# Second attention: each head's operands stacked on 64 partitions, and transposes issued just ahead of the weighting

## What is computed

```
q = xn @ wq.T + bq;  k = xn @ wk.T + bk_;  v = xn @ wv.T + bv      # 8 x 512 x 256
scores = einsum('bhsd,bhtd->bhst', q, k) / sqrt(16)                # per batch and head 512 x 512
attn = softmax(scores, axis=-1)
out = einsum('bhst,bhtd->bhsd', attn, v)
return out @ wo.T + bo
```

## Time and profile before

| what | value |
| --- | --- |
| median of 3 runs | 2060.38 us (2059.51 to 2063.23) |
| profiled execution, its own time | 2060.63 us |
| its span in the trace | 2058.9 us |
| PE busy | 1896.0 us, 92% |
| DVE busy | 1444.2 us, 70% |
| ACT busy | 1283.8 us, 62% |
| POOL busy | 649.4 us, 32% |

### The profile page before, as it was taken

One profiled execution on the slowest core, in us unless ns is written; L12 is line 12 of the kernel. 1 busy time (PEld: TensorE's weight loads), 2 busy tenths in 40 slices (PEclk: granted clock), 3 DMA queues, 4 the chain that ended last, 5 costly groups with the idle time before them and its releaser, 6 DMA issues. The chain is left out here.

```text
span 2058.9 us, 33528 instructions
## 1 busy us (share of the span) xinstructions
PE 1896.0 (92%) x12080; PEld 1468.2 (71%) x12080; DVE 1444.2 (70%) x2916; ACT 1283.8 (62%) x3061; POOL 649.4 (32%) x1021
## 2 busy tenths in 40 slices
PE   1999999999999999999999699975999999999997
PEld 1888878778878788888888588863656655655653
DVE  5786885977858858868678554425777777777773
ACT  3665674665756746657567564532677777777784
POOL 0353453543534535535435232222001011111112
PEclk9999999999999999999999899996999999999999
DMA  6110211111112111111111474302001011011001
GB/s 226 42 42 22 52 42 32 42 32 44 40 32 50 43 33 42 32 42 42 28 35 42 132 273 151 113 26 93 21 1 52 1 52 52 1 52 52 1 32 42
DMA packets 75748, 112.34 MB, mean 55 GB/s; under 512 B 8256, under 2 KB 49600, under 8 KB 75072
## 3 DMA queue, kind: packets, MB, share of 16 engines
q1 hardware_dynamic: 75040, 109.14, 18.1%
q10 hardware_dynamic: 544, 1.05, 0.2%
HBM read 55.64 MB, written 20.97 MB: 37 GB/s over the span
## 5 line engine op out<-in xcount | busy, mean ns | idle before, releaser
L1519 DVE TENSOR_REDUCE nm<-ps 128x1 f32<-128x512 f32 x512 | 336.8, 687 | 117.4 <-PE ps L1382 112.7
L1626 ACT ACTIVATE pt<-pst 128x512 f32<-128x512 f32 x512 | 296.9, 602 | 143.2 <-PE pst L1390 141.7
L804 POOL TENSOR_SCALAR pr<-pr,rinv 128x128 f32<-128x128 f32 (+3 forms) x512 | 264.1, 537 | 374.3 <-DVE rinv L692 374.3
L572 ACT ACTIVATE pr<-sc,nmax 128x128 f32<-128x128 f32 (+3 forms) x512 | 268.5, 527 | 143.4 <-DVE nmax L681 141.9
L681 DVE TENSOR_REDUCE nmax<-sc 128x1 f32<-128x128 f32 (+3 forms) x512 | 222.9, 483 | 76.7 <-PE sc L408 76.7
L1382 PE MATMUL ps<-kb,qb 96*128 96x512 f32 x512 | 238.9, 468 | 13.5 <-DVE nm L1519 11.1
L810 POOL TENSOR_TENSOR qk<-ra,rb 128x256 f32<-128x256 f32 x256 | 183.5, 739 | 206.6 <-DVE rb L703 170.8
L1390 PE MATMUL pst<-qb,kb 128*128 128x512 f32 x512 | 208.1, 408 | 6.7 <-ACT pt L1626 3.6
L1382 PEld LDWEIGHTS ps<-kb,qb 96*128 96x128 f32 x512 | 97.9, 192 | 145.4 <-issue 83.8
L420 PE MATMUL w<-ident,pr 128*128 128x128 f32 x1280 | 171.3, 281 | 25.7 <-DVE rb L703 19.8
L382 PE MATMUL w<-wq_hi,xt_hi 128*128 128x384 f32 x512 | 183.0, 358 | 2.4 <-DVE xt_lo L675 1.5
(11 more groups left out here) (205 smaller groups left out, 4558.5 us busy)
## 6 DMA issues: line engine op xcount, KB each, us to landing
k<-k SPq DMA_DIRECT2D x256, 128.0 KB, 2.2
raw<-in_w SPq DMA_DIRECT2D x16, 640.0 KB, 5.7
raw<-in_w SPq DMA_DIRECT2D x8, 704.0 KB, 4.2
xa<-in_x SPq DMA_DIRECT2D x2, 2048.0 KB, 13.8
x<-in_x SPq DMA_DIRECT2D x8, 512.0 KB, 3.9
x_scratch<-x SPq DMA_DIRECT2D x8, 512.0 KB, 2.9
xt_hi_scratch<-xt_hi SPq DMA_DIRECT2D x1, 4096.0 KB, 14.0
xt_lo_scratch<-xt_lo SPq DMA_DIRECT2D x1, 4096.0 KB, 22.9
```

The source lines that it names most:

```text
L572: act.activation(pr[:, h, SOFF[i]:SOFF[i] + (i + 1) * P], sc[:, bank, at:at + (i + 1) * P], ACT.Exp, bias=nmax[:, h, i:i + 1], accum_out=r ...
L804: pool.tensor_scalar(p, p, rinv[:, h, i:i + 1], 1.0, ALU.mult, ALU.mult).then_inc(scaled, 1)
L1519: dve.tensor_reduce(nm[:, g % 2, i, h:h + 1], ps[:, i % 2, :], AXX, ALU.max, negate=True).then_inc(max_done, 1)
L1626: act.activation(pt[:, g % 2, h, i, :], pst[:, i % 2, :], ACT.Exp).then_inc(exp_done, 1)
```

## The change

- S4 = 64: a head's stack gets a fourth 16-row part, in front. In `zq` it is zero, in `zk` it holds ones in two columns (set once by POOL), which takes over the work of `sel`. So two heads fill 128 rows, and each head has a 64-row half of its own in `qb` and in `kb`. `own` and `sel` and their setup go.
- `score` and `score_t` contract over 64 rows, the half of their head: `slice(h % 2 * S4, h % 2 * S4 + S4)`. In a pair the two stand in opposite halves, since their heads are h + 1 and h.
- ACT copies four stacks per group instead of six. DVE's `take_n` adds the turned maxima to all 128 rows of `qb` instead of copying 32 rows.
- PE's transposes no longer stand between pairs, but behind pair (h,3), ahead of `weigh`: `turn_z` j = 2, 3 of group q + 2 at the end of step 0, `turn_o` at the end of step 1, `turn_z` j = 0, 1 of group q + 3 at the end of step 3. `turn_n` stays.
- DVE's `take_o` moves from after (1,3) to after (2,0).
- The projections stand after all four pairs of step 2 of g = 1. `turn_on` moves to the end of step 2 of g = 2, with ACT's copies at (3,0), (3,1) and `split_ot` at (3,2). `out_project`, `take_out` move to step 2 of g = 3. POOL's `finish` stands after the split of g = 3. `on` gets a second buffer.

```diff
-    S3 = 3 * D1
+    S4 = 4 * D1
...
-        TURNS = ((0, 0), (0, 1), (0, 3), (1, 1))
-        STACKS = ((0, 0), (0, 1), (0, 3), (1, 0), (1, 1), (1, 2))
-        PROJECTIONS = ((1, 3), (2, 0), (2, 2), (2, 3))
+        STACKS = ((0, 0), (0, 1), (1, 0), (1, 1))
+        PROJECTIONS = ((2, 0), (2, 1), (2, 2), (2, 3))
...
+                pool.memset(zq[:, :, :, 0, :].bitcast(F32), 0.0).then_inc(pads_set, 1)
+                pool.memset(zk[:, :, :, 0, :].bitcast(F32), 0.0).then_inc(pads_set, 1)
+                pool.wait_ge(pads_set, 2)
+                for a in range(2):
+                    pool.memset(zk[:, :, 2 * a:2 * a + 2, 0, 2 * a:2 * a + 2].bitcast(F32), 1.0).then_inc(pads_set, 1)
...
-                        if g == 2 and not first:
+                        if g == 3 and not first:
                             finish(b - 1)
...
                 def score(q, g, h, i):
-                    if h < 2 and i == 0:
-                        pe.wait_ge(stack_done, 6 * q + (3 if h == 0 else 6))
+                    if h % 2 == 0 and i == 0:
+                        pe.wait_ge(stack_done, 4 * q + 3 + h // 2)
                     n = 16 * q + 4 * h + i
+                    rows = slice(h % 2 * S4, h % 2 * S4 + S4)
                     pe.wait_ge(max_done, n)
-                    pe.matmul(ps[:, i % 2, :], qb[0:2 * S3, g, h // 2, i * P:(i + 1) * P], kb[0:2 * S3, g, h, :],
+                    pe.matmul(ps[:, i % 2, :], qb[rows, g, h // 2, i * P:(i + 1) * P], kb[rows, g, h // 2, :],
                               start=True, stop=True).then_inc(s_done, 1)
 
                 def score_t(q, g, h, i):
                     if h == 0 and i == 0:
                         pe.wait_ge(n_done, 2 * q + 2)
                     n = 16 * q + 4 * h + i
+                    rows = slice(h % 2 * S4, h % 2 * S4 + S4)
                     pe.wait_ge(exp_done, n)
-                    pe.matmul(pst[:, i % 2, :], kb[:, g, h, i * P:(i + 1) * P], qb[:, g, h // 2, :],
+                    pe.matmul(pst[:, i % 2, :], kb[rows, g, h // 2, i * P:(i + 1) * P], qb[rows, g, h // 2, :],
...
-                            if (h, i) in TURNS and more2:
-                                j = TURNS.index((h, i))
-                                if j < 2 and g == 2 and not first:
-                                    bank_read = (ot_lo_done, NC * b)
-                                elif j < 2 and g == 3 and not first:
-                                    bank_read = (so_done, NT * b)
-                                else:
-                                    bank_read = (stack_done, 6 * (q + 2) + (-2, 0, 1, 2)[j])
-                                turn_z(q + 2, j, bank_read)
                             if (h, i) in PROJECTIONS and projects:
                                 if (h, i) == PROJECTIONS[0]:
                                     pe.wait_ge(xs_in, 32 * b + 64)
                                     pe.wait_ge(z_lo_done, 2 * q + 6)
                                 project(b + 1, PROJECTIONS.index((h, i)))
-                            if h == 1 and i == 2 and back2:
-                                turn_o(q - 2, q + 1)
-                            if h == HG - 1:
-                                if i == 1 and more1:
-                                    turn_n(q + 1)
-                                if g == 1 and not first and i >= 2:
-                                    if last:
-                                        pe.wait_ge(stack_done, 6 * (q + 2) + 3 + i)
-                                    else:
-                                        pe.wait_ge(qn_done, 2 * NT * (b + 1) + 5 + i)
-                                    turn_on(b - 1, i - 2)
-                                if g == 2 and not first:
-                                    if i < 2 and not last:
-                                        pe.wait_ge(stack_done, 6 * (q + 2) + 5 + i)
-                                    out_project(b - 1, i)
+                            if h == HG - 1 and i == 1 and more1:
+                                turn_n(q + 1)
+                            if h == 2 and g == 3 and not first:
+                                if i < 2 and more2:
+                                    pe.wait_ge(stack_done, 4 * (q + 2) + 3 + i)
+                                out_project(b - 1, i)
+
+                        if h == 0 and more2:
+                            for j in (2, 3):
+                                turn_z(q + 2, j, (stack_done, 4 * (q + 2) + j - 1))
+                        if h == 1 and back2:
+                            turn_o(q - 2, q + 1)
+                        if h == 2 and g == 2 and not first:
+                            for k in range(NC):
+                                if more2:
+                                    pe.wait_ge(stack_done, 4 * (q + 2) + 3 + k)
+                                turn_on(b - 1, k)
+                        if h == HG - 1 and more3:
+                            for j in range(2):
+                                if projects:
+                                    bank_read = (qn_done, 2 * NT * (b + 2))
+                                elif g == 2 and not first:
+                                    bank_read = (ot_lo_done, NC * b)
+                                elif g == 3 and not first:
+                                    bank_read = (so_done, NT * b)
+                                else:
+                                    bank_read = (stack_done, 4 * (q + 2) + 3 + j)
+                                turn_z(q + 3, j, bank_read)
...
-                        dve.tensor_copy(qb[2 * S3:P, g, a, :], pn[2 * D1 * a:2 * D1 * (a + 1), :]).then_inc(n_done, 1)
+                        dve.tensor_tensor(qb[:, g, a, :], pn[:], qb[:, g, a, :].bitcast(F32), ALU.add).then_inc(n_done, 1)
...
-                            if h == 1 and i == 3 and back2:
+                            if h == 2 and i == 0 and back2:
                                 take_o(q - 2, (g + 2) % NG1)
+                            if h == 2 and g == 3 and not first:
+                                take_out(b - 1, i)
                             if h == HG - 1:
                                 if i == 1 and more1:
                                     take_n(q + 1, (g + 1) % NG1)
-                                if g == 1 and not first and i == 3:
+                                if g == 2 and not first and i == 2:
                                     split_ot(b - 1)
-                                if g == 2 and not first:
-                                    take_out(b - 1, i)
...
-                    rows = slice(0, 2 * S3)
-                    if j < 2:
-                        act.wait_ge(z_turned, 4 * q + j + 1)
-                        act.copy(qb[rows, g, j, :], w[rows, j, :]).then_inc(stack_done, 1)
-                    else:
-                        h = j - 2
-                        act.wait_ge(z_turned, 4 * q + 3 + h // 2)
-                        act.mul(kb[rows, g, h, :], w[rows, h // 2, :], own[rows, h % 2:h % 2 + 1]).then_inc(stack_done, 1)
+                    act.wait_ge(z_turned, 4 * q + j + 1)
+                    act.copy((qb, kb)[j // 2][:, g, j % 2, :], w[:, j % 2, :]).then_inc(stack_done, 1)
```

76 lines of the change are left out of this document (29 added, 47 removed).

## The result

The changed kernel takes **2206.9 us** (median of 4 runs, 2197.9 to 2212.7) against 2061.6 for the kernel before (4 runs, 2059.5 to 2063.2): ratio **1.070, 95% interval 1.066 to 1.074**. It is 7% slower. The prediction had the direction and most of the mechanisms; its time, 2122, and its range up to 2152 were too low. The profiled execution has a span of 2202.4 and a time of 2204.7.

The account below looks back on a forecast made before the run. Plain steps were taken as bound by a loop through DVE (or ACT) and PE. Per full batch 8.2 us, 10.2 with the clock, 61 over batches 1 to 6, total +62 on 2060.6: 2122 us, range 2098 to 2152.

Parts of the forecast that it names:

- the sum's 8.2: Added time per full batch without the clock: 0.5 + 0 + 1.5 + 6.2 us for g = 0 to 3.
- Pairs start together: `score` and `score_t` in opposite 64-row halves: starts 0.10 us apart, saving 0.24 once per step.
- Step 2 at 3.93: Plain step 2: 3.54 - 0.24, plus 0.63 for DVE's `take_o` between its first two maxima; +0.4 us.
- Step 3 of g = 3 and POOL: DVE's third `take_out` waits for POOL's `finish`, behind the split; steps 2 and 3 together +5.7 us.
- Step 3 of g = 2 and split_ot: PE's `turn_z` waits for `split_ot`, behind `take_n` and a maximum on DVE: 5.4 us instead of 2.4, +3.0.
- 2.6 + 0.3 + 0.4 + 0.53 + 1.00: Plain step 0, last `score_t` at 2.6, then two turns ahead of the weighting: 4.8 us, +0.1.
- +0.1, hidden by `take_n`: Plain step 3: two turns ahead of the weighting make 2.4 us where `take_n` and a maximum set 2.3.
- 4 x (2.03 + 0.34): Step 2 of g = 1: four projections with pairs, plus 0.25 + 1.0, giving 10.7 us; group change about 0.
- The switch of rows: Rival: array drains at switches around pairs, 16 us in all, 2138; chance 0.18 together with pairs not overlapping.
- The clock: Falls of the granted clock in g = 3 and often g = 2, 1.4 and 0.6 us, raising 8.2 to 10.2.
- the clock falls in plain groups too: Rival: a fall costing 1.4 us in every second group makes 22 us, 2144; chance 0.12.
- Start and end: Program start -1.5 us from fewer copies, batch 0 +1, batch 7 +2.

Follow-up runs that it names:

- e4: Changed kernel with the earlier kernel's order put back in every engine, keeping its stacks, copies and 64-row halves: 2053.5 us, ratio 0.9964 to the kernel before.
- e2: Changed kernel with DVE's `take_o` issued behind the fourth maximum of step 1 again: 2174.8 us, ratio 1.055 to the kernel before.
- e1: Changed kernel with POOL's `finish` ahead of the next group's low parts in g = 3: 2184.3 us, ratio 1.059 to the kernel before.
- e3: Changed kernel with `score` and `score_t` over all 128 rows, so no row halves (scores differ): 2158.0 us, ratio 1.047 to the kernel before.
- e6: Changed kernel with the first three `score_t` of each step 2 and step 3 issued twice: 2194.8 us, ratio 1.066 to the kernel before.

## Why the prediction was wrong in size

The direction was right, and so were the two waits in their place and cause. Three terms of the sum failed. The transposes behind the last pair and the pairs among full-row products are most of the 4.7 us a batch by which all but the clock came out above the sum's 8.2. The clock cost some 6.1 a batch where it had 2.0. The start, batch 0 and the end cost 27 where it had 1.5. Point by point, by its own steps:

- **Pairs start together.** Right, and more so: 0.00 apart, where I took 0.10. e4 shows the gain as worked out, 0.24 a plain step.
- **Step 2 at 3.93.** Right to 0.01, and its cause too: e2 takes `take_o` out and 0.62 goes.
- **Step 3 of g = 3 and POOL.** The mechanism was right. DVE waited 4.96 with POOL as releaser, and step 3 took 10.28 against my 8.6. From start to start, `turn_n` took 1.04 where it takes 0.68 at full clock, the last pair 0.56 (0.48), the two transposes 1.90 (1.02) and the weighting 1.28 (1.00). That is 1.6, and without it the step has 8.7. e1 confirms the wait: 4.5 less.
- **Step 3 of g = 2 and split_ot.** Right: from the end of the second maximum 6.5 instead of my 5.4, of which 0.85 + 0.47 are the lower clock.
- **The switch and the transposes: mis-sized.** This is the first step that failed. In "2.6 + 0.3 + 0.4 + 0.53 + 1.00" the last `score_t` came at 2.69, from it to the turn took 0.43, and two turns 1.02 instead of 0.93; in step 1 it was 2.19, 0.43 and 0.59 against 2.1, 0.3 and 0.53. Each of these steps came out 0.25 to 0.35 above my number, and the plain group at +1.3 instead of +0.5. Of step 3, "+0.1, hidden by `take_n`" had the wrong cover: it is 0.25 longer by `score`, 4.44 against 4.19 in the rows below, and e4 shows that without the two turns it is 1.02 shorter from weighting to weighting. The order costs 0.07 + 0.49 + 0.63 + 1.02 = 2.2 a plain group, in steps 0 to 3 (e4 to after).

  The first `score` of step 3 of g = 0 and that of the next step, in the kernel before:

```profile
1680.13 0.50 PE L1382 MATMUL ps<-kb,qb 96*128 96x512 f32 x1
...
1684.32 0.47 PE L1382 MATMUL ps<-kb,qb 96*128 96x512 f32 x1 [0.53 <-DVE nm L1519]
```

- **A lone pair: wrong.** "4 x (2.03 + 0.34)" has 2.37 for each cycle, and it took 2.70 to 2.72, since a pair among projections takes 0.62 to 0.64 (2.70 or 2.72 less the 2.08 of a projection) and not 0.34: step 2 of g = 1 took 11.8 and not 10.7, and the group is 1.6 longer and not 0. In step 2 of g = 3 it is the same: the last `score_t` came 4.0 after the first `score` and not 3.2, with cycles of 1.33 (pair to output projection 0.43, six products 0.90, where I had some 0.7), and the step took 6.3 and not 5.2. The two steps together are 2.2 a batch, some 13 in six.
- **The switch of rows,** which I priced at 16 in all as a rival's term, is behind both points: e3, without it, has each of these places shorter by 0.06 to 0.15. Pair to pair takes 0.33, pair to transpose or projection 0.42 to 0.43, and a transpose of four between pairs 0.59 where two in a row take 0.43 for the second: 0.1 on one side and 0.16 on the other. The Trainium skill, TensorEngine Tiling, Key Properties, says that a change of tiling mode drains the engine. The traces agree that such a change costs time; that it is a drain no run shows. The Trainium skill, TensorE: Matmul & The Clock Gate, Part 3, has products of different row groups starting about 4 ns apart. The traces agree: 0.00 to 0.01 us here. I had given the second only a place in the range and the first only a rival, where both hold at once.
- **The clock: wrong.** I took 2.0 a batch, in the shadow of two waits. In the batch shown the clock is at its lower level for 17.1 us: 6.8 in g = 2 and 10.2 in g = 3. The six batches have 0.91 over 575.93 us. A fall that meets eight transposes costs 0.9 by them alone (1.87 instead of 1.02), and falls hit steps 0 of g = 2 and g = 3 whose waits are no longer than those of g = 0 (0.55 and 0.3). That is the rival "the clock falls in plain groups too", given 0.12, in part: in plain steps of g = 2 and g = 3, while g = 0 and g = 1 of this batch have 1.00. e3 and e6, which give PE more work, have fewer falls. My argument against it was one window of the earlier trace rows with 0.82 busy at clock 1.00; g = 0 of the changed kernel has 14.81 of 17.69 busy, 0.84, and no fall either, so a busy share over a group did not tell where the clock falls. What does stays open.
- **Start and end: wrong.** I had -1.5 at the start, +1 for batch 0 and +2 for batch 7. The first weighting comes 4.6 later, the rest of batch 0 takes 7.3 more, batch 7 up to its last weighting 12.3 more and what follows 2.9 more. The clock is 0.50 from 1420 to 1460 and from 2160 to 2180 (before, 0.50 to 1.00 in the former). e3, with clock 0.66 to 1.00 there, has its first weighting 4.1 earlier than the kernel before. That the clock is all of it is argued, not shown.

The sum a batch: step 0 of g = 2 and of g = 3 took 1.6 more than the 5.14 of g = 0, and the two steps 3 had 1.3 and 1.6 of lower clock, 6.1 in all, where I had 2.0. What is left, 95.6 - 6.1 - 76.6 = 12.9, stands against my 8.2: +0.8 in g = 0, +1.6 in g = 1, +0.6 in g = 2, +1.7 in g = 3. These 8.8 us in six batches are 53 of the 81 us missed (143.5 more in span, where I had 62). Start, batch 0 and batch 7 make 26 more, and the first of the six batches was 2.6 longer than the one shown.

## What to carry to other kernels

Where a step is a loop through two engines, ask of each moved instruction on which side of the last product it lands: behind the last pair `turn_o` cost a step 0.17 or 0.49 more than between the pairs, and step 3 paid 1.02 for two transposes, while in a step without slack between the pairs moving them there gave nothing. In this kernel, sharing the array by row halves paid only where such pairs follow one another (0.33 against 0.47); one between products of full rows costs more than two full-row products (0.62 to 0.64 against 0.47), so count the two cases apart. Joining lone pairs afterwards gave little here, 0.34 a batch, and nothing in g = 1. And when a change makes PE idle, price the clock over the whole batch and not only behind the waits.

## What was not expected of the hardware

- Two products in different 64-row halves start 0.00 to 0.01 apart and a pair of 512 columns costs 0.33, so 0.7 of two full-row products.
- Giving PE 144 needless products in the six batches did not make the kernel slower (median 2194.8 against 2206.9, ranges that overlap), while the granted clock rose from 0.91 to 0.94 in these batches. Leaving out its longest wait (e1) did not raise the clock: 0.88 in the six batches of the profiled run, and 0.934 to 0.947 over the whole program in the four runs, against 0.935 to 0.945.
- Around PE's waits of 2.33 and 3.09 us the clock was at its lower level, 1.2 GHz, for 3.4 and for 6.8 us: eight transposes take 1.87 to 1.90 instead of 1.02, and the weighting 1.28 to 1.47 instead of 1.00.
